# Linear attention of a four-layer mixer: key exponentials times the normalised rows, Wv once per layer, and turned rows kept in memory for the queries

## The reference, cut to what matters

```python
def _layernorm(x, g, b):
    mu = x.mean(-1, keepdims=True)
    var = ((x - mu) ** 2).mean(-1, keepdims=True)
    return (x - mu) * jax.lax.rsqrt(var + EPS) * g + b

def _linear_attn(x, Wq, Wk, Wv, Wo, bo):      # 8 heads of 32 columns
    q = softmax(split(x @ Wq) * scale, axis=-1)   # over the 32 columns of a head
    k = softmax(split(x @ Wk) * scale, axis=-2)   # over the 3125 rows
    v = split(x @ Wv)
    context = einsum('bhnd,bhne->bhde', k, v)
    out = einsum('bhnd,bhde->bhne', q, context)
    return join(out) @ Wo + bo

for i in range(4):
    h = _layernorm(x, ln1_g[i], ln1_b[i])
    x = x + _linear_attn(h, Wq[i], Wk[i], Wv[i], Wo[i], bo[i])
    h = _layernorm(x, ln2_g[i], ln2_b[i])
    x = x + (gelu(h @ W1[i] + b1[i]) @ W2[i] + b2[i])
```

## Time and profile before

| what | us |
|---|---|
| runs, median of 3 (lowest, highest) | 2359.34 (2351.77, 2360.32) |
| profiled execution, its own time | 2356.42 |
| its span, first to last instruction | 2354.7 |
| PE busy | 1992.1 (85%) |
| DVE busy | 1524.8 (65%) |
| POOL busy | 1373.6 (58%) |
| ACT busy | 925.8 (39%) |
| mean granted TensorE clock | 0.936 |

### The profile page before, as it was taken

How to read it: one execution, slowest core, us unless ns; L and a number is a source line. 1 busy time by engine, 2 the same in 40 slices (tenths; PEclk the granted TensorE clock), 3 DMA queues, 4 the chain that set the end, 5 groups by cost and what they waited for, 6 DMA issues and landing times.

```text
span 2354.7 us, 33082 instructions
## 1 busy us (share of the span) xinstructions
PE 1992.1 (85%) x10654; PEld 1640.4 (70%) x10654; DVE 1524.8 (65%) x3442; ACT 925.8 (39%) x1947; POOL 1373.6 (58%) x1125
## 2 busy tenths in 40 slices
PE   2359899999888999988899998889999785799990
PEld 1337677777776778877677787767778574788880
DVE  4758867776787777678767777876766457411116
ACT  1224444443444444444444434454444231233330
POOL 4156566677556666756666675666667501566650
PEclk7769999999999999999999999999999885899995
DMA  8652222233322233333222233322223521799997
GB/s 212 183 148 72 69 71 71 73 78 101 87 72 70 72 74 75 85 104 76 67 73 73 71 84 105 89 72 73 70 72 84 118 77 44 236 305 303 302 280 169
DMA packets 269780, 268.49 MB, mean 114 GB/s; under 512 B 146075, under 2 KB 203486, under 8 KB 269630
## 3 DMA queue, kind: packets, MB, share of 16 engines
q0 software_dynamic: 127488, 134.76, 23.7%
q1 hardware_dynamic: 138030, 131.85, 19.1%
q10 hardware_dynamic: 4112, 0.03, 0.1%
HBM read 230.37 MB, written 35.05 MB: 113 GB/s over the span
## 4 chain that ended last, share of the span: by engine, by line
PE 58%; DVE 18%; DMA 10%; ACT 5%; issue 5%; POOL 2%; SPq 2%; DVEq 1%; POOLq 0%; ACTq 0%
PE bank L1205 21%; PE bank L1314 14%; PE bank L433 3%; DVE zl L455 3%; PE bank L434 3%; PE bank L441 3%; DMA xs<-zn_d,slot_tok 2%; PE bank L1215 2%; PE bank L1432 2%; DMA aT<-attr_d 2%; PE bank L1254 2%; PE bank L1440 2%; DVE z L481 2%; ACT zr L449 1%; DMA y_d<-yo,slot_row 1%
## 5 line engine op out<-in xcount | busy, mean ns | idle before, releaser
L843 POOL DMA_INDIRECT G<-P_d,src_T x896 | 1141.9, 1274 | 658.5 <-DVE z L481 388.6
L481 DVE TENSOR_TENSOR z<-bank,G 125x512 f32<-125x512 f32 x448 | 288.4, 685 | 174.4 <-PE bank L441 122.0
L1205 PE MATMUL bank<-W_s,hid 128*125 128x256 f32 x1600 | 366.6, 383 | 26.3 <-DVE qe L1616 26.3
L449 ACT ACTIVATE zr<-z 125x512 fp32r<-125x512 f32 x448 | 266.4, 629 | 304.8 <-DVE z L481 272.6
L455 DVE SCALAR_TENSOR_TENSOR zl<-z,zr 125x512 fp32r<-125x512 f32 x448 | 295.9, 702 | 130.4 <-ACT zr L449 125.9
L1314 PE MATMUL bank<-TT,W_s 128*128 128x250 f32 (+1 forms) x1280 | 352.9, 428 | 0.0
L1205 PEld LDWEIGHTS bank<-W_s,hid 128*125 128x125 f32 x1600 | 296.2, 190 | 73.5 <-issue 30.8
L1314 PEld LDWEIGHTS bank<-TT,W_s 128*128 128x128 f32 x1280 | 238.0, 191 | 93.9 <-issue 2.3
L433 PE MATMUL bank<-zr,onehot 125*125 125x256 f32 x896 | 268.2, 332 | 29.5 <-DVE zl L455 29.3
L1013 ACT ACTIVATE hid<-bank,b_s 128x375 f32<-128x375 f32 x320 | 166.6, 522 | 191.4 <-PE bank L1314 167.2
L434 PE MATMUL bank<-zl,onehot 125*125 125x256 f32 x896 | 227.0, 284 | 0.0
(11 more groups left out here) (313 smaller groups left out, 3019.6 us busy)
## 6 DMA issues: line engine op xcount, KB each, us to landing
W_s<-in_L_ffn_w SPq DMA_DIRECT2D x64, 512.0 KB
hid<-in_L_ffn_w SPq DMA_DIRECT2D x64, 512.0 KB
G<-P_d,src_T POOLq DMA_INDIRECT x896
W_s<-in_L_mix_W SPq DMA_DIRECT2D x8, 1024.0 KB, 10.5
aT<-attr_d SPq DMA_DIRECT2D x224, 31.2 KB
attr_d<-hn SPq DMA_DIRECT2D x12, 246.1 KB, 3.7
X<-in_x SPq DMA_DIRECT2D x5, 560.0 KB
P_d<-es SPq DMA_DIRECT2D x25, 112.0 KB
```

Of the source, the lines that this page charges most:

```text
L449: nc.scalar.activation(zr[:, s, k, :], z[:, k, :], ACT.Relu).then_inc(r_done, 1)
L481: nc.vector.tensor_tensor(z[:, k, :], edge_bank[k][0:ET, :], G[:, ST * s + 2 * k:ST * s + 2 * k + 2, :].rearrange("p j d -> p (j d)"), ALU ...
L843: pool.indirect_dma_start(G[:, j, :], None, P_d[:, :], bass.IndirectOffsetOnAxis(ap=src_T[:, at:at + 1], axis=0)).then_inc(g_in[j], 16)
L1205: ins = pe.matmul(to[0:T, (j - a) * D:(j - a) * D + D], w, m, start=n == 0, stop=n == len(pairs) - 1)
```

## The change: what it does

The values are no longer computed. With E the exponentials of the keys and n the normalised rows before gain and shift, E'v = (E'n)(gain) Wv + (sum E)(shift) Wv. So stage K multiplies es by the normalised rows themselves, 256 columns for each half in place of 129, and the sum of the exponentials comes from ACT's accumulator (`piece_sum`) and two small DVE additions a piece (`key_sum`). For this the normalised rows of two groups live at once (hn and hn2, which takes V5's place). In stage M the summed rows are divided by the sum of the keys, turned (ctxN to ctxF, with gain and shift on ACT), multiplied by Wv, masked (ctxT) and multiplied by Wo.

The first norm's turned rows are written to DRAM (nT_d, 128 partitions of 1252 floats, 641 KB a group) when TT has been filled for the keys, and read back into TT for the queries. So stages M and P compute no first norm again. In stage K the last group has no normalising at all.

The core of the diff:

```diff
-        V5 = sb("V5", [T, GT, KD, 129])
+        hn2 = sb("hn2", [T, GT, D])
+            def keep_normalised_T(l, g):
+                if g == 0:
+                    sp.wait_ge(nT_in, l * NG * 16)
+                sp.wait_ge(ring_act, ring_h1(l, g) + LNU + 1)
+                sp.dma_start(nT_d[g], TT[:, :, :].rearrange("p k n -> p (k n)")).then_inc(nT_out, 16)
+            def load_normalised_T(g):
+                sp.dma_start(TT[:, :, :].rearrange("p k n -> p (k n)"), nT_d[g]).then_inc(nT_in, 16)
             for l in range(L):
-                attr_steps(step_k(l, 0) + (PG if l == 0 else 0), step_k(l, NG) + 1)
+                keep_normalised_T(l, 0)
+                at = step_k(l, 0) + (PG if l == 0 else 0)
+                for g in range(NG):
+                    attr_steps(at, step_k(l, g + 1))
+                    at = max(at, step_k(l, g + 1))
+                    if g + 1 < NG:
+                        keep_normalised_T(l, g + 1)
+                sp.wait_ge(ring_full, ring_k(l, NG - 1) + 4)
+                sp.wait_ge(nT_out, (l * NG + NG) * 16)
+                load_normalised_T(0)
+                attr_steps(at, at + 2)
+                sp.wait_ge(row_full, row_q(l, 0) + NRP)
+                load_normalised_T(1)
...
+                for g in range(NG - 2):
+                    attr_steps(at, step_p(l, g) + 5)
+                    at = step_p(l, g) + 5
+                    sp.wait_ge(ring_full, ring_p(l, g) + 2 * NF)
+                    load_normalised_T(g + 2)
# ScalarE, stage K
-                                           bias=nb[:, pc, h:h + 1], scale=SCALE).then_inc(ring_act, 1)
+                                           bias=nb[:, pc, h:h + 1], scale=SCALE, accum_out=piece_sum[:, pc, h:h + 1]).then_inc(ring_act, 1)
-                    first_norm(u0 + 4, u0 + 4 - RING_A)
+                    if g + 1 < NG:
+                        act.wait_ge(nT_out, (l * NG + g + 1) * 16)
+                        first_norm(u0 + 4, u0 + 4 - RING_A)
# TensorE, stage K
-                        for i in ((0, 1), (2,))[pc]:
-                            rows_at(r0, i, lambda j: [(TT[:, k, tt_cols(j)], Wv_s[:, k, :]) for k in range(KD)])
...
-                                ins = pe.matmul(to[:, 129 * h:129 * h + 129], es[:, j, 128 * h:128 * h + 128], V5[:, j, h, :],
+                                ins = pe.matmul(to[:, D * h:D * h + D], es[:, j, 128 * h:128 * h + 128], NORM[g % 2][:, j, :],
# TensorE, stage M
+                step(eM + 1)
+                pe.wait_ge(ring_act, uM + 2)
+                to = row_of(rM + NRP)
+                for h in range(KD):
+                    for k in range(KD):
+                        ins = pe.matmul(to[:, 128 * h:128 * h + 128], Wv_s[:, k, 128 * h:128 * h + 128], ctxF[:, k, 128 * h:128 * h + 128],
# VectorE, stage K
-                    dve.wait_ge(ring_full, u0)
-                    normalised((g + 1) % NG)
+                    if g + 1 < NG:
+                        normalised(g + 1, NORM[(g + 1) % 2])
...
+                        dve.tensor_tensor(key_sum[:, :], key_sum[:, :], corr[:, pc, :], ALU.mult).then_inc(key_summed, 1)
+                        dve.tensor_tensor(key_sum[:, :], key_sum[:, :], piece_sum[:, pc, :], ALU.add).then_inc(key_summed, 1)
# stages M and P
-                queries(0)
-                dve.wait_ge(ring_full, ring_q1(l, 0) + LNU)
-                normalised(1)
+                queries(0)
...
-                    if g + 2 < NG:
-                        dve.wait_ge(ring_full, ring_h2(l, g) + LNU)
-                        normalised(g + 2)
...
-                        if g + 2 < NG:
-                            queries(g + 2, (0,))
                         step(e0 + 4)
                         if g + 2 < NG:
-                            queries(g + 2, (1, 2))
+                            queries(g + 2)
```

162 lines of the change are left out of this document (80 added, 82 removed).

## The result

The changed kernel takes 2439.24 us, median of four runs (2437.61 to 2443.16); the kernel before, run beside it, took 2358.34 (2351.77 to 2360.32). The ratio is 1.035, 95% interval 1.033 to 1.037: 3.5% slower. The forecast was 2388 with a range up to 2418. The direction was right, the size was 51 us off, and the time lies outside the range.

A forecast was written before the change was run, and what follows sets the result against it. PE held 58% of the chain of waits, with DVE nearly as long in stage K. Four layers at +2.9 (11.6), layer changes 13.2 and clock 8 gave +33 us on 2356.4: 2388, range 2335 to 2418.

The forecast's parts named there:

- Stage K, inner groups: Groups 1 to 3 of each layer: DVE waits for wider products, PE for the first exponential; +4.6 us a layer.
- The walk: Following the waits from one edge matmul to the next in an inner stage K: 18.7 us instead of about 17.1.
- Stage K, last group: No normalising, transposes or TT writes there, but maxima wait for later keys: -1.4 us, bounds 0 and -2.4.
- Stage M: Longer chain to the first attention addition (+3.3) and wider context work (+1.0), less one normalising (-1.87): +2.3 us a layer.
- Seams: Three changes of layer: nT_d's transfer delays aT and ACT's TT writes, PE idles over 6 us; +4.4 us each.
- ACT may not write TT before this transfer has landed: At a change of layers, ACT waits for group 0's rows to reach DRAM, holding PE's edge matmul: another 1.1 us.
- Stage P: Transposes, TT writes and normalising go: -0.95 us for each of three groups, +0.25 for the last; -2.6 a layer.
- TensorE's clock: Half speed after PE's idle, charged 1.3 us in about six of 16 stages K: +8 us, bounds 0 and +27.
- The third rival: The clock falls in nearly every stage K, 27 us instead of 8, with dearer layer changes: 2412 us, chance 0.18.
- The draw: Inner stages K gain and lose nothing and the clock stays: 2363 us, no change; chance 0.15.
- PE sets the end everywhere: DVE has unseen slack in stage K, so PE's 65 us saving shows: 2313 us, faster; chance 0.14.
- the signs that I named: Expected in the trace: inner stages K about 18.5 us, named PE, DVE and ACT waits, stage P about 1 us shorter.

The follow-up runs named there:

- narrow products: Changed kernel with the exponentials' products and DVE's additions to ctxS cut from 256 to 128 columns, half the sums left out: 2410.88 us, ratio 1.019.
- first unit put back: Changed kernel with the queries' first unit in stages M and P made ahead of the fourth step again: 2414.43 us, ratio 1.022.
- memory part: Kernel before, values and 129-column products kept, with the first norm's turned rows written to DRAM and read back for the queries: 2340.17 us, ratio 0.993.

## Why the prediction was right and wrong

- **Stage K, inner groups: the mechanism was right.** PE's idle for the first exponential (1.78 us), DVE's wait at its second ctxS (0.52) and the order are there. PE's second pause, 1.47 us, the walk did not name. The walk gave +1.6, +1.4, +1.6; at full clock it is +1.1, +1.5, and +1.4 to +2.0. The narrow products show that the width has 1.1 us or more of it in most of these stages. With the clock as it fell, the changed kernel has +2.8, +2.8, +3.0.
- **Stage K, last group:** forecast -1.4. At full clock it is 16.5 us (in the kernel with the first unit put back) for 17.2, so -0.7. Where the clock falls in it, as in three of four layers of the changed kernel, it is 18.3, +1.1.
- **Stage M:** forecast +2.3 a layer, measured +9.1 for four. The number is right, in part by luck: from the start of the softmax's last operation to the first attention addition it is 10.8 us for 6.3, +4.5 where the walk had +3.3, and M has 15 us more at 1.2 GHz, for which nothing was charged. What made up for it is open.
- **Seams:** forecast +4.4, measured +5.8, +4.5 and +7.0. The step "ACT may not write TT before this transfer has landed" was right and was the last to end; its transfer's 12.90 us replaced the 11.73 of the earlier trace rows. Its place behind the weights is worth 3.0 us a seam. The forecast idle of 6 us or more is there as 3.59, 1.17 and 3.93, the first of them DVE's longer chain. The clock is at 0.75 in this stage; how much of the seam that is, no run parts. Where nothing was ahead of it the store landed in 3.5 us and the loads in 4.6, the forecast's 2.1 and 2.5, and no load made PE wait.
- **Stage P: the step that failed in its sign.** Forecast -2.6 a layer, measured +3.1. The first norm gone is worth 1.6 us a stage (61.8 before, 60.2 with the memory part at a clock of 1.00; the forecast had 0.95 net). Moving the unit costs 1.0 to 1.3 while the forecast's 0.95 leaves it 0.65 at most. And where the clock falls behind the wait, it takes another 1.7 (61.9 at 0.97 for 60.2 at 1.00). I had not charged P for the clock at all.
- **TensorE's clock: the step that failed most.** "1.3 us for about six of the 16 stages K" became 137 us at 1.2 GHz in the stages K, in 19 of 20, and in P 35 us more than before. The third rival, "the clock falls in nearly every stage K", was the true case; what I held against it, that no pause is longer than 2 us, was no argument: the clock fell behind pauses of 1.78 and 1.47 us. Its 27 us for K were near: unused matmuls took away 16 us with 103 of the 137 us at 1.2 GHz, which by that ratio is 21 for all of it, an estimate that is low by what these matmuls cost. It missed P.
- **The sum:** of the 51 us missed, 23 are in K (34 forecast, 57 measured), 23 in P (-10 for +12), and 5 ahead of the layers. K's 57 are 33 in the inner stages (18 forecast), 3 in the last ones (-6), 17 at the seams (13) and 4 in the first stage of the first layer, for which the forecast had no term; its 8 for the clock belong to all of them.
- **The chances:** slower had 0.71. The rival that came true had 0.18 and was priced without P, so that its 2412 was 27 us low and the range ended below the result.
- **The draw and "PE sets the end everywhere"** are refuted by the same row: an inner stage K of 20.1 us, over the 17.1 from which DVE's chain decides. At full clock it is still 18.5 or more.
- **What showed it:** of the signs that I named, these are there: PE standing for the first exponentials, DVE waiting at ctxS, ACT's wait of 4.12 us for nT_d ahead of TT, no wait of PE for nT_d's loads. Four came out otherwise: the inner stage K is 20.1 us and not 18.5, the 6 us of idle at a seam came in three pieces, the first attention addition comes 9.3 us behind the softmax of the queries (724.93 to 734.22) and not 8, and stage P did not get shorter. The granted clock by stage was not among my signs and should have been the first.

## What to carry to other kernels

Work that fills a wait can be more than free: it can keep TensorE's clock up. Before removing matmuls from a stage, look at whether they fill a wait, and charge every stage in which a pause of a microsecond or two takes their place with what the clock takes there (here 1.7 us in a stage P, and 1.3 to 1.5 in a stage K), stage P as well as K. Where such a pause can't go, a few unused matmuls inside it pay, but only so many as the wait has room for. And split a change before judging it: here one half was worth -0.7% (-1.5% once its transfer and one wait were set right), and the other +2.7%.

## What the runs showed of the hardware

- The cost of a removed instruction can be negative: 400 matmuls fewer, 21 us more.
- 8 unused matmuls (16 instructions, 1.95 us) in a wait of 2.15 us took away the 1.2 GHz time of the second and third stage P in every layer. Without them six of these eight stages had it and two had not, with the same waits (0.42 and 2.13 us). A fall of 3.4 us costs 1.7 us there (61.9 for 60.2).
- A transfer of 641 KB to DRAM landed 3.5 us after its issue in the median, a load back 4.6 us. Behind 2.56 MB of weights the same store took 12.90, and SP needed 3.34 us only to issue it.
- The accumulator's read behind an activation shows as 0.19 to 0.20 us here too, the figure of the earlier trace rows, and partly overlaps the activation before it.
